# The expert layer of a perceiver: three fp32r products in place of one fp32 product, with each expert's weights fetched once

## The reference, cut to what matters

```
xf = layernorm(x).reshape(1024, 512)
scores = softmax(xf @ w_gate)                 # 8 experts
weights, idx = top_k(scores, 2)               # each token goes to 2 experts
exp_x[expert, position] = xf[token]           # tokens sorted by expert
h = einsum('ecd,edf->ecf', exp_x, c_fc)       # 512 -> 1536, all in float32
a, g = split(h, 2)
h = silu(a) * g                               # 768
exp_out = einsum('ecf,efd->ecd', h, c_proj)   # 768 -> 512
out = sum over the 2 experts of weight * exp_out[expert, position]
```

## Time and profile before

| | us |
|---|---|
| median of three runs | 2249.49 |
| the profiled execution | 2252.86 |
| its span in the trace | 2251.0 |
| expert layer, routing block | 333 to 393 |
| expert layer, 23 tiles | 393 to 799 |
| gather and change to cross-attention | 799 to 817 |

### The profile page before, as it was taken

How to read it: one execution, slowest core, us unless ns; L and a number is a source line. 1 busy time by engine, 2 the same in 40 slices (tenths; PEclk the granted TensorE clock), 3 DMA queues, 4 the chain that set the end, 5 groups by cost and what they waited for, 6 DMA issues and landing times. The chain is left out here.

```text
span 2251.0 us, 29109 instructions
## 1 busy us (share of the span) xinstructions
PE 2014.5 (89%) x9936; PEld 1418.6 (63%) x9936; DVE 1085.9 (48%) x2233; ACT 914.2 (41%) x1684; POOL 100.5 (4%) x113
## 2 busy tenths in 40 slices
PE   7978963999999959999999999999968898858998
PEld 5647763555555547777778787878746676623443
DVE  5665651001010127363544445363538899929852
ACT  5743320111111125353544444454526667726650
POOL 0000002000000001000000000000000000002220
PEclk9989875999999989999999999999988888779999
DMA  7410006777777622110101100000212000020000
GB/s 266 135 46 1 0 17 245 289 313 312 293 297 313 261 71 76 38 47 14 47 14 47 43 31 33 28 33 28 75 63 103 1 1 1 1 80 1 5 10 24
DMA packets 33156, 208.19 MB, mean 92 GB/s; under 512 B 4546, under 2 KB 4674, under 8 KB 25540
## 3 DMA queue, kind: packets, MB, share of 16 engines
q1 hardware_dynamic: 30532, 199.02, 23.5%
q0 software_dynamic: 2560, 8.39, 1.1%
HBM read 186.95 MB, written 20.45 MB: 92 GB/s over the span
## 5 line engine op out<-in xcount | busy, mean ns | idle before, releaser
L109 PE MATMUL PS<-cT,qs 128*128 128x512 f32 x1152 | 293.9, 401 | 9.0 <-ACT pb L1259 7.0
L109 PE MATMUL PS<-pT,cN 128*128 128x512 f32 x1152 | 271.8, 394 | 1.7 <-DVE pT L1354 1.7
L109 PEld LDWEIGHTS PS<-cT,qs 128*128 128x128 f32 x1152 | 208.6, 188 | 59.3 <-issue 15.0
L917 PE MATMUL PS<-W,xgT 128*128 128x384 f32 x736 | 243.7, 490 | 1.4 <-ACT xgT L940 1.4
L109 PEld LDWEIGHTS PS<-pT,cN 128*128 128x128 f32 x1152 | 215.1, 189 | 45.8 <-DVE pT L1354 1.9
L917 PEld LDWEIGHTS PS<-W,xgT 128*128 128x128 f32 x736 | 141.1, 192 | 104.4 <-issue 12.1
L109 PE MATMUL PS<-ws,xT 128*128 128x512 f32 x672 | 180.4, 427 | 6.4 <-DVE ws L563 4.9
L109 PEld LDWEIGHTS PS<-ws,xT 128*128 128x128 f32 x672 | 137.6, 207 | 45.8 <-issue 11.5
L1349 DVE TENSOR_REDUCE nmax<-PS 128x1 f32<-128x512 f32 x128 | 87.7, 685 | 156.0 <-PE PS L109 155.6
L968 DVE TENSOR_TENSOR hid<-gated,PS 128x384 f32<-128x384 f32 x46 | 23.4, 551 | 278.4 <-PE PS L893 235.6
L1254 ACT ACTIVATE qp<-PS 128x512 f32<-128x512 f32 x96 | 57.4, 598 | 191.4 <-PE PS L109 191.4
(11 more groups left out here) (231 smaller groups left out, 3096.5 us busy)
## 6 DMA issues: line engine op xcount, KB each, us to landing
W<-in_fc SPq DMA_DIRECT2D x23, 3072.0 KB, 12.4
W<-in_proj SPq DMA_DIRECT2D x23, 1536.0 KB, 6.5
cT<-in_ctxT SPq DMA_DIRECT2D x16, 768.0 KB, 5.2
ct_in<-in_ctxT SPq DMA_DIRECT2D x16, 768.0 KB, 4.2
cn_in<-in_ctxN SPq DMA_DIRECT2D x16, 768.0 KB, 5.1
W<-in_w SPq DMA_DIRECT2D x2, 4096.0 KB, 12.9
routed_x<-zero SPq DMA_DIRECT2D x23, 256.0 KB, 5.4
xg<-routed_x SPq DMA_DIRECT2D x23, 256.0 KB, 5.6
```

The costliest lines, as they stand in the source:

```text
L109: mm = nc.tensor.matmul(out, lhs(m, s), rhs(n, s), start=(opens and (s, m, n) == terms[0]), stop=((s, m, n) == terms[-1]))
L917: mm = nc.tensor.matmul(ps[c][:, 0:HFE], xgT[:, k, :], fc[u][:, k, c * HFE:(c + 1) * HFE], start=(k == 0), stop=(k == DK - 1))
```

## The change

Both products of the expert layer become split products.

- **Weights.** SP loads every expert's weights once, into two raw buffers that take turns: `raw_fc`, which lies in `W0`, and `raw_pj`. The first two experts are loaded at the start of the routing block. Expert e is loaded when the last tile of expert e-2 has been split (a wait against a count from the new table `edge`). The cross-attention weights share `W0`, so their load moves from the routing block to the end, behind the last split.
- **Splitting.** There is one split copy of the weights, `fw` (two parts, 4 column groups) and `pw` (two parts, 2 halves). Each tile makes it anew: ScalarE the rounded part, VectorE the rest, six pieces of 128x1536 per tile on each of the two engines. The `fc` pieces are made one tile ahead, each as soon as the tile before has used its group. The rows `xgT` and `hT` are split too. Which raw buffer a tile reads comes from a new table `parity`, read into a register (`value_load`, L889), and ScalarE also reads `owner` (L979) for its wait on the load.
- **Order.** PE runs hidden groups 0 and 1, the transposes of the tile before, groups 2 and 3, the transposes of the next tile's rows, and the output product of the tile before. Copying `y` moves from VectorE to ScalarE. The loads of `xg` and stores of `y` move from SP to GpSimd.

The core of the diff:

```diff
-        xn = sbuf("xnall3", [P, NT, D])
-        fc = [W1[:, u * 9216:u * 9216 + NFC].rearrange("p (k n) -> p k n", k=DK) for u in range(2)]
-        pj = [W1[:, u * 9216 + NFC:(u + 1) * 9216].rearrange("p (k n) -> p k n", k=FK) for u in range(2)]
+        raw_fc = W0[:, 0:2 * NFC].rearrange("p (u k n) -> p u k n", u=2, k=DK)
+        raw_pj = sbuf("raw_pj3", [P, 2, FK, D])
...
+        def load(sp, ex):
+            u = ex % 2
+            if ex:
+                sp.wait_ge(s_fc, BASE + 16 * ex)
+            sp.dma_start(raw_fc[:, u], a["fc"][ex]).then_inc(s_fc, 16)
+            if ex:
+                sp.wait_ge(s_pj, BASE + 16 * ex)
+            sp.dma_start(raw_pj[:, u], a["proj"][ex]).then_inc(s_pj, 16)
...
-                    for dst, name in ((e.wq4, "wq4"), (e.wk4, "wk4"), (e.wv4, "wv4"), (e.wo4, "wo4")):
-                        sp.dma_start(dst, a[name]).then_inc(e.s_w4, 16)
-                    sp.wait_ge(s_owner, BASE + 1)
-                    load_fc(sp, 0, sp.value_load(owner[0:1, 0:1], min_val=0, max_val=NE - 1))
+                    load(sp, 0)
+                    load(sp, 1)
...
             @block.sync
+                for ex in range(2, NE):
+                    end = sp.value_load(edge[0:1, ex - 2:ex - 1], min_val=0, max_val=ET)
+                    u = ex % 2
+                    sp.wait_ge(s_fc, BASE + 16 * ex)
+                    sp.wait_ge(fc_lo, end * 4 + BASE)
+                    sp.dma_start(raw_fc[:, u], a["fc"][ex]).then_inc(s_fc, 16)
+                    sp.wait_ge(s_pj, BASE + 16 * ex)
+                    sp.wait_ge(pj_lo, end * 2 + BASE)
+                    sp.dma_start(raw_pj[:, u], a["proj"][ex]).then_inc(s_pj, 16)
+                sp.wait_ge(s_fc, BASE + 16 * NE)
+                sp.wait_ge(s_pj, BASE + 16 * NE)
+                sp.wait_ge(fc_lo, BASE + 4 * ET)
+                for dst, name in ((e.wq4, "wq4"), (e.wk4, "wk4"), (e.wv4, "wv4"), (e.wo4, "wo4")):
+                    sp.dma_start(dst, a[name]).then_inc(e.s_w4, 16)
...
             @block.tensor
+                def hidden(s, c):
+                    pe.wait_ge(x_lo, BASE + s + 1)
+                    pe.wait_ge(fc_lo, BASE + 4 * s + c + 1)
+                    if not is_(s, 0):
+                        pe.wait_ge(silu_sb if c < 2 else hid_sb, BASE + 2 * s + c % 2 - 1)
+                    split_product(nc, ps[c][:, 0:HFE], lambda part, k: xgT[part][:, k, :],
+                                  lambda part, k: fw[part][:, k, fc_cols(c)], DK).then_inc(f_mm, 1)
...
+                def step(s, u, pair):
+                    hidden(s, 0)
+                    hidden(s, 1)
+                    if not is_(s, 0):
+                        turn_h(s - 1)
+                    hidden(s, 2)
+                    hidden(s, 3)
+                    if not is_(s, ET - 1):
+                        turn_x(s + 1, 1 - u, pair + u)
+                    if not is_(s, 0):
+                        out_proj(s - 1)
...
             @block.scalar
+                def first_fc(s, c, par):
+                    if not is_(s, 0):
+                        act.wait_ge(f_mm, BASE + 4 * s + c - 3)
+                    nc.scalar.activation(fw[0][:, :, fc_cols(c)], raw_fc_of(par, c), ACT.Copy).then_inc(fc_hi, 1)
...
             @block.vector
+                def rest_fc(s, c, par):
+                    ve.wait_ge(fc_hi, BASE + 4 * s + c + 1)
+                    rest(fw[1][:, :, fc_cols(c)], raw_fc_of(par, c), fw[0][:, :, fc_cols(c)]).then_inc(fc_lo, 1)
...
             @block.gpsimd
+                for s in range(ET):
+                    if s >= 2:
+                        pool.wait_ge(x_mm, BASE + s - 1)
+                    nc.gpsimd.dma_start(xg[:, s % 2, :], xg_d[s * P:(s + 1) * P, :]).then_inc(xg_in[s % 2], 16)
+                    if s >= 2:
+                        store(s - 2)
```

More of the change, by code:

```diff
@@ L902, in out_proj @@
                     mm.then_inc(y_mm, 1)
                 def step(s, u, pair):
-                    pe.wait_ge(xg_in[u], BASE + 16 * pair + 16)
-                    pe.wait_ge(xgT_sb, BASE + s)
-                    for k in range(DK):
-                        tr = nc.tensor.transpose(ps[4][:, k * P:(k + 1) * P], xg[:, u, k * P:(k + 1) * P], ident)
-                    tr.then_inc(tr_mm, 1)
-                    if not (isinstance(s, int) and s < 2):
-                        out_proj(s - 2, u, pair - 1)
@@ new lines, in _ @@
+                par = parity_of(act, 0)
+                loaded(0, s_fc)
+                first_fc(0, 0, par)
+                first_x(0)
+                for c in range(1, 4):
+                    first_fc(0, c, par)
+                steps(act, step)
+                y_take(ET - 2, 1, (ET - 2) // 2)
+                par = parity_of(act, ET - 1)
+                loaded(ET - 1, s_pj)
+                first_pj(ET - 1, 0, par)
+                first_h(ET - 1, 0)
+                first_h(ET - 1, 1)
@@ new lines, in rest_x, with rest_h @@
+                def rest_x(s):
+                    ve.wait_ge(x_hi, BASE + s + 1)
+                    hi, lo = (part[:, :, :].rearrange("p k t -> p (k t)") for part in xgT)
+                    rest(lo, ps[4], hi).then_inc(x_lo, 1)
+                def rest_h(s, g):
+                    ve.wait_ge(hT_hi, BASE + 2 * s + g + 1)
+                    hi, lo = (part[:, pj_rows(g), :].rearrange("p f t -> p (f t)") for part in hT)
+                    rest(lo, ps[5 + g][:, 0:HF * P], hi).then_inc(hT_lo, 1)
@@ new lines, in product @@
+                def product(s, c):
+                    ve.wait_ge(silu_sb, BASE + 2 * s + c + 1)
+                    ve.wait_ge(f_mm, BASE + 4 * s + c + 3)
+                    if not is_(s, 0):
+                        ve.wait_ge(hT_mm, BASE + 2 * s + c - 1)
+                    nc.vector.tensor_tensor(hid[:, fc_cols(c)], gated[:, fc_cols(c)], ps[2 + c][:, 0:HFE],
+                                            ALU.mult).then_inc(hid_sb, 1)
+                def step(s, u, pair):
+                    first, last = is_(s, 0), is_(s, ET - 1)
+                    if not first:
+                        par_p = parity_of(ve, s - 1)
+                        rest_pj(s - 1, 0, par_p)
+                    if not last:
+                        par = parity_of(ve, s + 1)
+                        rest_fc(s + 1, 0, par)
+                    if not first:
+                        rest_h(s - 1, 0)
+                        rest_h(s - 1, 1)
+                        rest_pj(s - 1, 1, par_p)
+                    product(s, 0)
+                    if not last:
+                        rest_fc(s + 1, 1, par)
+                    product(s, 1)
+                    if not last:
+                        rest_x(s + 1)
+                        rest_fc(s + 1, 2, par)
+                        rest_fc(s + 1, 3, par)
```

229 lines of the change are left out of this document (130 added, 99 removed).

## The result

The changed kernel takes 2178.9 us in the median of its runs (2176.6 to 2178.9). The ratio to the kernel before is 0.967, with a 95% interval of 0.9655 to 0.9684 (the two medians alone give 0.9686). One further run of each kernel was far slower (2704 and 7015 us) and is left out. Forecast were 2178 us and a range of 2156 to 2218. The profiled execution has a span of 2177.1 us, 73.9 less than before.

The account below looks back on a forecast made before the run. PE's passes bound the tiles; 399.5 + 12 + 21 x 13.8 + 22.4 = 723.7 against 798.94 before, net -73.7 us after small additions, so 2252.9 becomes 2179, stated as 2178 us, range 2156 to 2218.

Parts of the forecast that it names:

- The bound: Expert tiles before the change: PE's passes set the 17.25 us period; fetching weights once saves no time by itself.
- PE's work: PE per tile: 48 matmuls at 0.173, 18 at 0.228 and 1.1 of transposes, 13.5 us against 16.7 before.
- The lower bound by columns: PE's 384-column matmuls: same cost per column as 512-column ones gives at least 0.171 us each; 0.173 was taken.
- rival 2: Split product on PE slower than its columns: 0.228 us at 384 columns, period 16.4, total 2235 us; chance 0.12.
- The 0.3 us of short waits: Added to PE's 13.5 us per tile for short waits between engines, making a period of 13.8 us.
- Elementwise sums: ScalarE's and VectorE's work per tile: 12.0 and 13.45 us with pieces alone, 11.0 and 12.65 back to back.
- The round: Chain through PE, ScalarE and VectorE in a tile: PE finds each piece in time, with 0.7 us room at `xgT`.
- rival 1: Elementwise engines set the tile period, 14.3 to 15.3 us: 11 to 32 us more, about 2200; chance 0.22.
- Hidden transfers: GpSimd's `xg` loads hidden by 0.8 us, expert weights hidden, cross-attention weights hidden with 22 us of room.
- Start and end: Expert stage's ends: hidden product starts at about 399.5 us, first tile takes 12 us, last tile 22.4 us.
- Before and behind the tiles: Five more small VectorE operations in routing add 0.5 us; GpSimd's issue of the last store adds 1 us.
- Rival 3: GpSimd holds up VectorE's weight rests, +0.96 us each, total 2285 us; chance 0.04 together with other ways to be slower.

Follow-up runs that it names:

- experiment 2: Changed kernel, all splitting kept, but both products as one fp32 product of the rounded parts: 2252.73 us, ratio 1.0002 to the kernel before.
- experiment 1: Kernel before, but each weight load from the third tile on fetches only 64 columns: 2252.87 us, ratio 1.0001.
- experiment 5: Changed kernel with one more 128x1536 subtraction per tile on VectorE, ahead of the rest of piece 3: 2192.55 us, ratio 0.973 to the kernel before.
- experiment 3: Changed kernel with two passes in place of three in both expert products, all splitting kept: 2158.24 us, ratio 0.9579 to the kernel before.
- experiment 4: Changed kernel with one more 128x1536 subtraction per tile on VectorE, ahead of the rest of piece 0: 2215.93 us, ratio 0.9826 to the kernel before.
- Experiment 8: Changed kernel without register loads on ScalarE, VectorE and SP in the tiles, only two experts' weights fetched: 2176.82 us, ratio 0.9657 to the kernel before.
- experiment 7: Changed kernel with one more 128x1536 copy per tile on ScalarE, ahead of piece 3: 2180.15 us, ratio 0.9677 to the kernel before.
- experiment 6: Changed kernel with the rests of `pw` made for the first tile only: 2176.27 us, ratio 0.9657 to the kernel before.

## Why the prediction was right

**The bound.** "The stage is bound by PE's passes", and "fetching weights once saves no time by itself": experiments 2 and 1 show them, with ratios of 1.0002 and 1.0001.

**PE's work.** Forecast 8.3 + 4.1 + 1.1 = 13.5, measured 48 x 0.177 + 18 x 0.233 + 0.9 = 8.5 + 4.2 + 0.9 = 13.6. Both kinds start 2% further apart than I took them. The lower bound by columns was the near one; rival 2 (0.228 at 384 columns) is dead by the rows of PE alone. The estimate of 0.216 at 512 columns, from the Trainium skill's "TensorE: Matmul & The Clock Gate", section "Back-to-back issue gap", is for an isolated matmul; it is 7% under the 0.233 seen here in a row of them.

**The 0.3 us of short waits.** Wrong in size: they are 0.07 in the mean, on a period of 13.63, not 13.8. Over 21 periods that is 286.3 us in place of 289.8, 3.5 less. Terms too low on PE's work and too high on waits offset each other in part.

**Elementwise sums.** 12.0 and 13.45 alone, 11.0 and 12.65 back to back; measured busy 10.7 to 10.9 and 12.35 to 12.4. The back-to-back figures were the right ones, because the queues rarely run dry. With VectorE full or nearly so, its own work is 12.47 (experiment 5, without the added operation) to 12.6 (experiment 3).

**The round.** This step failed in size. I gave it 0.7 us of room at `xgT` and took 0.9 by the sums when I wrote the expectation of experiment 4; the room measured there is 0.1. What was missing is in the waits: I took ScalarE's register loads as hidden (at worst "the part above its short neighbour", 0.7 us), but 1.5 us of them stand idle. The tile of the kernel after that ends hidden group 3 at 568.43 us shows it against the prediction's times: the first half of `pw` ends at 7.7 (forecast 7.4), then come 0.65 us of idle time at the second pair of loads, which my round did not have at all, so piece 0 ends at 10.2 (9.6), and the rest of `xgT` at 17.9 (17.3), both 0.6 late. PE wants it at 18.1 and gets it 0.24 after its end: no room is left in this tile. Experiment 8 agrees, with 1.24 us of room once loads and fetches are gone. The step failed, and the forecast came out right by luck, because a round of 13.45 still lies under PE's 13.56. Another 0.2 us on it, and rival 1 would have begun.

**Hidden transfers.** GpSimd's direct issue takes 0.54 us, not 0.957, and `xg` lands in 3.2 us (median), not 5.6. Weights are hidden, as said. The cross-attention's are issued at 698.8 to 700.1 us, land 8.0 to 19.5 us later and are wanted at 741: hidden with 22 us, as said. That they would be in the way of the store behind a shorter last tile, I had not seen; it costs nothing in this kernel.

**Start and end.** First hidden product 6.1 us after the first load (forecast 6.3), first tile 12.3 (12), both right. The last tile takes from its hidden product at 695.61 to 720.83 = 25.2 us, not 22.4. Two terms of its last chain were missing. The row of 18 matmuls takes 5.97 us behind the pause, where 4.3 are the price at full clock, which I had used: 1.7. And the first half of `pw` waits 0.72 for its register loads, which I had left out. The remaining 0.4 are handovers. So 6.1 + 12.3 + 286.3 + 25.2 = 330.0 against 330.5 in the forecast: 3.5 too much in the periods and 2.8 too little at the end. That these cancel is luck, and so is the last microsecond of the total: the sum was made for the profiled execution (2252.9 to 2179, measured 2178.9), while the medians differ by 70.6 us and not by 73.7.

**Before and behind the tiles.** +0.5 was forecast for the routing, and +0.25 came. Behind the tiles +1 was forecast, +2.67 came: 0.5 between `y` and the gather, and 2.1 between VectorE's last operation and the next layer. The row for the latter is "DVE st L134 <- PEq", 6.73 us here and 4.64 before. It has 6.73 to 6.85 in every trace of a kernel made from the changed one and 4.50 to 4.64 in both made from the one before, so it belongs to the change. The instructions in that place are the same, and no experiment addresses it: its cause is open.

**Rival 3.** VectorE's rests have a mean of 1755 ns, as the 1.76 of one alone, beside two GpSimd issues per tile. Of the contention that the Trainium skill names in "GPSIMD Engine Reference", section "Specifications", nothing shows beside this kind of work; the tiles have no GpSimd arithmetic to test the rest of it.

## What to carry to other kernels

When work is moved from the bound engine to idle ones, make two sums and not one: each engine's busy time per period, back to back, and the longest round of waits through several engines. The smaller of the two margins holds for an added operation only by its place; here 0.1 us on the round and 1.1 off it. And when a tail is shortened, look at what the DMA engines do in the new place of its transfers before counting the gain.

## What the runs showed of the hardware

- fp32r matmuls at full clock start every 0.177 us with 384 columns and 0.233 with 512, which is the same per column within 1.5%; their weight loads show no floor at these widths.
- Register loads are not hidden on ScalarE: a pair left it idle for 0.7 to 0.9 us (`pw`) and 0.5 to 0.7 (`fw`), behind operations of 0.5 to 0.6 us. One load between two issues of SP took 0.45; whether a load costs ScalarE more than SP is not shown, since its overlap with the operation ahead is not known.
- Behind 4.66 us of idle time TensorE had a mean granted clock of 0.58 for 3 us and 0.85 for the next 3; 18 matmuls took 5.97 us, which take 4.3 without a pause. The same pause was followed by 0.50 (the 1.2 GHz level) for 3 us in experiments 5 and 7, and the row took 7.24 and 6.84 us; so the price of one pause varies by 1.3 us between traces. Behind 3.27 us (experiment 6) the clock was 0.53 for 3 us and the row took 5.69; behind 1.45 us of idle time the clock was 1.00.
- A store of 256 KB took 4.24 us to the gather behind it with the DMA engines at work on other transfers (4.37 in the other execution of that kernel), and 2.54 or 2.55 without.
